# Graph attention on images: the order in which SyncE asks for its loads in a slot

## The reference

```
alpha = relu(bn(wa x)), sigma = relu(bn(ws x))            # 32 hidden channels each
att   = softmax over m of (alpha_n . sigma_m), only the 8 spatial neighbours m of pixel n
h_s   = att x                                             # per pixel
Gc    = x x^T over pixels; catt = softmax over d of Gc, only the channels d = c - 1 and c + 1
h_p   = catt x
out   = (1 - gama) x + gama elu(h_s + h_p)
```

## Time and profile before

| | us |
|---|---|
| median of 3 runs | 413.83 (413.4 to 425.62) |
| profiled execution | 416.75 |
| its span, first to last instruction | 415.0 |
| mean granted clock of TensorE | 0.964 of full speed |
| HBM read, written | 103.26 MB, 33.55 MB |

### The profile page before, as it was taken

How to read it: one execution, slowest core, us unless ns; L and a number is a source line. 1 busy time by engine, 2 the same in 40 slices (tenths; PEclk the granted TensorE clock), 3 DMA queues, 4 the chain that set the end, 5 groups by cost and what they waited for, 6 DMA issues and landing times.

```text
span 415.0 us, 14346 instructions
## 1 busy us (share of the span) xinstructions
PE 364.1 (88%) x5487; PEld 277.5 (67%) x5488; DVE 315.5 (76%) x1072; ACT 305.8 (74%) x900; POOL 291.6 (70%) x198
## 2 busy tenths in 40 slices
PE   5977998989998999999899999999989898999783
PEld 1546767666766867676686767677676667767662
DVE  1166978778787688879768887978788697888775
ACT  2178686868878497887849788787869678686761
POOL 2007686787868588787858878788868858787861
PEclk9889999999999899999989999999999899999778
DMA  8999999999999899999999999999999999985213
GB/s 274 414 368 404 315 344 357 366 359 347 364 346 385 292 358 366 388 364 351 356 317 337 382 385 360 363 378 383 342 367 358 365 307 367 341 297 202 103 53 152
DMA packets 40613, 137.74 MB, mean 332 GB/s; under 512 B 3296, under 2 KB 3552, under 8 KB 36448
## 3 DMA queue, kind: packets, MB, share of 16 engines
q1 hardware_dynamic: 40256, 136.76, 91.4%
q10 hardware_dynamic: 288, 0.07, 0.1%
HBM read 103.26 MB, written 33.55 MB: 330 GB/s over the span
## 4 chain that ended last, share of the span: by engine, by line
PE 32%; DMA 30%; DVE 20%; ACT 9%; issue 7%; SPq 0%; DVEq 0%; ACTq 0%
DMA upper<-x_t_dram 28%; PE gb L468 17%; PE z L468 11%; ACT score L281 6%; DVE probs L374 5%; DVE elu L389 5%; PE tr L543 3%; DVE z L383 3%; ACT z L301 3%; DMA x<-x_dram 2%; DVE gb L404 1%; DVE band L400 1%; DVE row_inv L370 1%; DVE pair_inv L420 1%; DVE catt L421 1%
## 5 line engine op out<-in xcount | busy, mean ns | idle before, releaser
L468 PEld LDWEIGHTS z<-probs_t,upper 64*128 64x128 f32 x2304 | 155.6, 191 | 44.6 <-issue 28.8
L468 PE MATMUL z<-probs_t,upper 64*128 64x128 f32 (+1 forms) x2304 | 173.5, 284 | 5.1 <-ACT probs_t L292 2.4
L247 POOL TENSOR_TENSOR blend<-elu,blend 128x1024 f32<-128x1024 f32 x62 | 146.2, 2358 | 9.5 <-POOL elu L243 0.4
L243 POOL TENSOR_SCALAR elu<-elu,vec,mix 128x1024 f32<-128x1024 f32 x62 | 74.0, 1193 | 98.5 <-DVE elu L389 98.5
L308 ACT ACTIVATE elu<-z 128x512 f32<-128x512 f32 x128 | 69.6, 597 | 60.6 <-PE z L468 60.6
L389 DVE SCALAR_TENSOR_TENSOR elu<-elu,z 128x512 f32<-128x512 f32 x124 | 79.5, 683 | 28.7 <-ACT elu L308 28.3
L301 ACT ACTIVATE z<-x,catt 128x512 f32<-128x512 f32 x128 | 83.6, 693 | 14.2 <-DVE catt L421 14.1
L281 ACT ACTIVATE score<-score,neg_max 128x128 f32<-128x128 f32 x256 | 86.2, 337 | 7.4 <-DVE neg_max L365 7.3
L383 DVE SCALAR_TENSOR_TENSOR z<-near,catt,z 128x512 f32<-128x512 f32 x128 | 90.3, 751 | 1.5 <-ACT z L301 1.5
L237 POOL TENSOR_SCALAR blend<-x,mix 128x1024 f32<-128x1024 f32 x64 | 72.0, 1126 | 6.5 <-DMA x<-x_dram 6.5
L468 PE MATMUL gb<-x,wt 128*32 128x256 f32 (+2 forms) x720 | 65.1, 480 | 2.5 <-DMA x<-x_dram 2.5
(11 more groups left out here) (49 smaller groups left out, 145.0 us busy)
## 6 DMA issues: line engine op xcount, KB each, us to landing
x<-x_dram SPq DMA_DIRECT2D x32, 1024.0 KB, 9.1
near<-x_near_dram SPq DMA_DIRECT2D x64, 512.0 KB, 7.8
out_dram<-blend SPq DMA_DIRECT2D x62, 512.0 KB, 8.0
upper<-x_t_dram SPq DMA_DIRECT2D x16, 1152.0 KB, 8.4
upper<-x_t_dram SPq DMA_DIRECT2D x16, 1024.0 KB, 7.9
out_dram<-blend SPq DMA_DIRECT2D x4, 256.0 KB, 2.1
const<-constants_dram SPq DMA_DIRECT2D x1, 291.5 KB, 12.0
const<-constants_dram SPq DMA_DIRECT2D x1, 128.0 KB, 2.2
```

What stands on the lines that cost most here:

```text
L243: nc.gpsimd.tensor_scalar(elu[s % 2][:, :, :], elu[s % 2][:, :, :], vec[:, V_GAMA:V_GAMA + 1], mix[:, 1:2], ALU.mult, ALU.add).then_inc(ga ...
L247: nc.gpsimd.tensor_tensor(blend[s % BLENDS][:, :, :], elu[s % 2][:, :, :], blend[s % BLENDS][:, :, :], ALU.add).then_inc(blend_done, 1)
L468: return nc.tensor.matmul(o, l, r, start=start, stop=stop, skip_group_check=True, **kw)
```

## The change

In each slot SP asks for the big block (`upper` or x) right after the waits at the slot's head, then waits for `z_half`, and then asks for the neighbour channels. The store stays last. Sizes, buffers, semaphores, the waits inside the helpers and the requests ahead of the loop are the same.

```diff
                     sp.wait_ge(score_done, t - t % 2 + 2)
                     if t > 0:
                         sp.wait_ge(pt_done, t)
-                if b + 1 < B:
-                    load_near(b + 1, q)
-                if t > 0 and real(t):
-                    sp.wait_ge(z_half, t)
-                if q % 2 == 0 and b + 2 < B:
-                    load_x(b + 2, q // 2)
                 if q == 1 and b + 1 < B:
                     load_by_key(b + 1, 1)
                 if q == 3 and b + 2 < B:
                     load_by_key(b + 2, 0)
+                if q % 2 == 0 and b + 2 < B:
+                    load_x(b + 2, q // 2)
+                if t > 0 and real(t):
+                    sp.wait_ge(z_half, t)
+                if b + 1 < B:
+                    load_near(b + 1, q)
                 if real(t - 2):
                     store(t - 2)
```

## The result

The changed kernel takes 395.51 us (median of 4 runs, 394.86 to 396.90) where the kernel before took 414.82 in four runs: ratio 0.955, 95% interval 0.950 to 0.960. It is faster by 4.5%.

A forecast was written before the change was run, and what follows sets the result against it. DMA engines set the pace in most images, with late block, low clock and late requests added in some. Gains 1.5 + 4.9 + 0.6 = 7.0 us take 416.75 to 409.8, about 407 in medians; range 397 to 416.

The forecast's parts named there:

- What bounds the kernel: Steady images: DMA engines set the pace in most, 24.03 us each, against 22.75 for compute without the wait.
- The step that failed: Request for upper in q = 1, 3.1 us earlier: gains only the bytes it overtakes, 1.5 us, and only once.
- The overtaken neighbours: The big block passes one near request of 0.524 MB in the DMA line: 1.5 us gained, once.
- The disturbed images: Images with late block, low clock and late requests, DMA share below full: their idle DMA time is regained, 4.9 us.
- the extra requests in q = 3: 1024 KB of upper asked for before gram_band: 2.9 us of DMA work while PE waits, counted towards the 4.9 us.
- The last image: Image from 351.73, before the tail: only the late request makes PE wait, and that wait goes, 0.6 us.
- The waits inside the moved requests: Waits in load_by_key and load_x, where SP could stand: all have passed already, so none costs anything.
- the neighbours asked for later: near requests go out after z_half, up to 3.9 us later; read one image later, so they cost nothing.
- PE bound: Rival: the wait for upper goes for good, every image takes 22.75 us; 395 us (394.5 in medians), chance 0.25.
- Slower: reads right behind a store: Rival: upper comes right behind a store and is slowed, images of 24.48 us; 418 us, chance 0.10.
- The bytes bind everywhere: Rival: the DMA line keeps its present mean rate whatever the requests do, only 2.1 us gained; 412 us, chance 0.22.
- My own signs: If right: images about 23.6 us, PE still waiting 5 to 12 us for upper, which lands 10 us or more after request.

The follow-up runs named there:

- the order alone: Against the changed kernel: the z_half wait comes first again, then the big block, then the neighbours; 418.6 us, ratio 0.998 to the kernel before.
- Earlier alone: Against the kernel before: neighbours first as before, then at once the big block without waiting for z_half; 402.6 us, ratio 0.958.
- spare loads: Against the changed kernel: 256 KB more to load in each slot, into tiles that nobody reads; 407.7 us, ratio 0.971 to the kernel before.

## Why the prediction was wrong, point by point

- **What bounds the kernel: half right.** That the start of `gram_band` is the tick, that only the second half of `upper` is waited for, and the pace of 22.75 us without that wait: all held (22.68). "It is the DMA engines that set the pace in most images" was wrong. I read it from a share of 1.00, from the image from 183.11 with 357 GB/s at 1.01, and from the page's 91.4%, which I called the part "of what 16 DMA engines could give"; it is the time that packets were open, and says nothing of what more could pass.
- **The step that failed** is the sentence "With the DMA share at 1.00, asking earlier only puts it at an earlier place in a line that moves at its own rate", and with it "it is worth that *once*". The line was not full: 411 to 415 GB/s pass when there is more to do. An earlier request lands earlier by nearly as much (2.6 of 3.1 us), in each image. Of the 3.1 us the line took back 0.5, not 1.6 in the first image and all of it from then on. The 14 portions of wait, which I warned against counting, are exactly what was gained: 12.6 us, and behind them 5.7 of shorter matmuls, 4.4 of it by the clock.
- **The overtaken neighbours, 1.5 us: not there.** With the order alone the wait was 16.5 us and the landing 8.5, no better than before; the times alone (0.998, 0.968 to 1.027) would not exclude 1.5 us. Earlier alone, which overtakes nothing, gave the gain.
- **The disturbed images, 4.9 us: near in size, by luck.** Their low clock did vanish, 4.4 us of slower matmuls in three images. It went in the kernel that moves q = 1 alone, together with the waits, so the extra requests in q = 3 were not needed; with those and the x requests alone the ratio is 0.996, and one image was still disturbed.
- **The last image, 0.6 us: right**, as far as it goes: its wait of 0.59 is gone, with all the others.
- **The waits inside the moved requests, and the neighbours asked for later: right.** SP stood inside the moved x requests for POOL 13 times, 6.0 us in all and 0.5 at most, where I had said that all these waits have passed; nothing waits for those loads in the steady part, and it costs no time. Neither `near` nor a store shows up among the waits of DVE or POOL.
- **The rivals.** "PE bound" had the right time and the right sign of how to see it, at a chance of 0.25. Its reason, reads that stall less at the head of the line, is not shown: the order alone did not shorten the landing (8.5 us). And my argument against it, "more requests can't fill what is full", is the failed step again. "Slower: reads right behind a store" is ruled out by the result. "The bytes bind everywhere" fails with 377 and 411 GB/s. The rule of the Trainium skill (DMA: Bandwidth & Descriptors, Where 436 GB/s comes from) that about 358 GB/s on the HBM side bind would have held the time at 411; the trace doesn't agree, with 377 GB/s through 13 images of the changed kernel and 411 with spare loads, and the measurement decides.
- **My own signs would have told it.** I wrote that `upper` lands 10 us after its request or more if I am right, "not less". It landed after 8.9.

What the trace of before could have shown: at a share of 1.01 or 1.02 three images carried 376, 357 and 382 GB/s. I took the spread for a change of the rate at which the engines can work, where most of it was slack. It was a hint and no proof: without any computing, at shares of 1.02 and 1.03, stretches of 50 us still had 380 and 415.

## What to carry to other kernels

A DMA share near 1 says that packets were open, not that no more could pass: put GB/s beside it, compare it with the best stretch, or add loads that nobody reads and see whether the time moves. When an engine waits for a load in every round, the compute pace in the good rounds is known, and the GB/s leave room, count the full wait times the rounds for an earlier request, up to the compute pace, before arguing it away with the queue. And find the one request that is waited for: here one of twelve per image, moved by 3.1 us, was all of a change in four slots.

## What the runs showed of the hardware that was not expected

- Loads and stores in this mix (103 MB read, 34 MB written) pass at 414 to 415 GB/s over 50 us stretches on one core, at a share of 1.03, and at 396 over the whole span without computing; at a share of 1.00 the kernel before moved 356.
- Even with landing times of 16.9 us, so with a long line, there was one stretch of 50 us with 380 GB/s at a share of 1.02. Why is open.
- To overtake 512 KB in the queue did not make the block land sooner (8.5 us against 8.4; ratio 0.998, 0.968 to 1.027), while some 1.2 us of earlier request took the wait of 14.8 us down to 3.9.
